# A four-level wavelet layer: input rows dealt four to a partition, and the forward transform split into 32x32 TensorE tiles over four images at once

## What is computed

```
def _L0_conv_ref(x, w_yl, w_yh):
    yl, yh = _dwt2(x, 4)
    yl_out = jnp.einsum('bixy,ioxy->boxy', yl, w_yl)
    yh_out = yh[:-1] + [jnp.einsum('bicxy,iocxy->bocxy', yh[-1], w_yh)]
    return _idwt2(yl_out, yh_out)
```

## Time and profile before

| | us |
|---|---|
| median of 3 runs | 2176.98 (2175.05 to 2181.13) |
| the profiled execution | 2176.45 |
| its span, first to last instruction | 2174.7 |
| last image's `h_stage` begins | 760.85 |
| first step of the mix begins | 773.15 |
| first store of the second pass | 885.15 |

### The profile page before, as it was taken

How to read it: one execution, slowest core, us unless ns; L and a number is a source line. 1 busy time by engine, 2 the same in 40 slices (tenths; PEclk the granted TensorE clock), 3 DMA queues, 4 the chain that set the end, 5 groups by cost and what they waited for, 6 DMA issues and landing times.

```text
span 2174.7 us, 30813 instructions
## 1 busy us (share of the span) xinstructions
PE 2006.3 (92%) x10540; PEld 824.1 (38%) x10540; DVE 846.7 (39%) x1615; ACT 506.2 (23%) x1079; POOL 3.6 (0%) x7
## 2 busy tenths in 40 slices
PE   8999999999999967999989889889889889889886
PEld 3344343434434345444333333333333333333332
DVE  2222222222222233455544444444444444444443
ACT  2222222222222268212112112112112112112110
POOL 0000000000000000000000000000000000000000
PEclk9999999999999989999999999999999999999998
DMA  9999999999999968699999999999999999999999
GB/s 382 409 363 361 346 357 360 349 363 347 356 353 352 349 244 316 246 384 408 409 409 409 409 409 409 409 409 409 409 409 409 409 409 409 409 409 409 408 409 396
DMA packets 406629, 827.10 MB, mean 380 GB/s; under 512 B 12752, under 2 KB 13520, under 8 KB 406608
## 3 DMA queue, kind: packets, MB, share of 16 engines
q1 hardware_dynamic: 406608, 826.80, 100.9%
HBM read 558.32 MB, written 268.44 MB: 380 GB/s over the span
## 4 chain that ended last, share of the span: by engine, by line
DMA 48%; PE 8%; SPq 5%; issue 2%; ACT 1%; DVEq 0%; ACTq 0%; DVE 0%
DMA out<-x_sb 46%; PE ps L455 5%; SPq L278 5%; PE ps L445 1%; DMA both<-w_full 1%; ACT both L541 1%; PE ps L411 1%; DMA x_sb<-x 1%; DMA both<-w_rest 1%; PE ps L406 0%; PE ps L435 0%; SPq L273 0%; ACT mix_sb L548 0%; SPq L272 0%; DVEq L134 0%
## 5 line engine op out<-in xcount | busy, mean ns | idle before, releaser
L455 PE MATMUL ps<-spread,const 128*128 128x512 f32 x2048 | 940.9, 602 | 111.2 <-DVE x_sb L690 111.2
L690 DVE TENSOR_TENSOR x_sb<-ps,x_sb 128x1024 f32<-128x1024 f32 x500 | 592.4, 1221 | 668.2 <-DMA x_sb<-x 593.3
L455 PEld LDWEIGHTS ps<-spread,const 128*128 128x128 f32 x2048 | 372.4, 189 | 679.2 <-issue 402.2
L327 PE MATMUL ps<-x_sb,const 128*64 128x512 f32 x2048 | 495.0, 604 | 8.8 <-DMA x_sb<-x 8.8
L595 ACT COPY spread<-ps 84x512 f32<-84x512 f32 x256 | 149.0, 582 | 970.1 <-PE ps L445 969.7
L646 DVE COPY work<-ps 128x80 f32<-128x80 f32 x256 | 61.9, 242 | 560.2 <-PE ps L337 560.2
L494 ACT COPY work<-ps 128x512 f32<-128x512 f32 x256 | 150.2, 587 | 537.4 <-PE ps L327 537.4
L445 PE MATMUL ps<-const,pick 128*84 128x512 f32 x512 | 261.3, 592 | 0.7 <-issue 0.7
L327 PEld LDWEIGHTS ps<-x_sb,const 128*64 128x64 f32 x2048 | 130.0, 137 | 205.9 <-issue 189.7
L337 PEld LDWEIGHTS ps<-const,work 128*128 128x128 f32 x1024 | 107.0, 140 | 207.2 <-issue 206.1
L337 PE MATMUL ps<-const,work 128*128 128x128 f32 x1024 | 167.8, 286 | 0.1
(11 more groups left out here) (22 smaller groups left out, 262.7 us busy)
## 6 DMA issues: line engine op xcount, KB each, us to landing
x_sb<-x SPq DMA_DIRECT2D x498, 1024.0 KB, 12.6
out<-x_sb SPq DMA_DIRECT2D x250, 1024.0 KB, 13.2
both<-w_full SPq DMA_DIRECT2D x30, 896.0 KB, 6.5
work<-x SPq DMA_DIRECT2D x6, 1024.0 KB, 9.9
out<-work SPq DMA_DIRECT2D x6, 1024.0 KB, 11.7
both<-w_rest SPq DMA_DIRECT2D x6, 224.0 KB, 3.9
const<-consts SPq DMA_DIRECT2D x1, 912.0 KB, 4.7
```

The source lines that it names most:

```text
L327: last = nc.tensor.matmul(ps[64 * j:64 * j + 64, p], const[:, AH + 64 * k:AH + 64 * k + 64], x_sb[:, c, k], start=k % 2 == 0, stop=k % 2 == 1)
L455: last = nc.tensor.matmul(ps[:, 2 + k], const[:, SH + P * k:SH + P * k + P], spread[:, p], start=True, stop=True)
L690: nc.vector.tensor_tensor(part, ps[:, 2 + 2 * half:4 + 2 * half], part, ALU.add).then_inc(added[half], 1)
```

## The change

- An image lies in SBUF as [128, 4, 512] with rows 4 p to 4 p + 3 in partition p. The four rows are adjacent in HBM too, so that each load and store of an image moves one run of 8 KB to a partition. In the built program the access is `[[2048, 128], [1, 2048]]` on both sides, the same form as the weight loads have. The constants of the second pass (`SH`) are dealt to match; its code is otherwise the same.
- `h_stage(a, t)` handles four images at once. It applies only the first three levels (low-pass) along the height, where 128 rows of input touch at most 25 outputs. So each 32-partition group g of the array takes its own 128 rows, and each 32-column group another image m: 64 matmuls of 32 rows by 32 columns, streaming 512. Output of (g, m) goes to PSUM quadrant (g + m) mod 4 of bank m.
- `turn_stage` is now a product instead of a transpose: along_h (128x128 as weights) times the fourth level's matrix `A4` (84 columns streamed). It turns the data, and sums the four windows in PSUM. VectorE's four instructions become one copy.
- `w_stage` applies three levels along the width: four matmuls of 32 columns, streaming 336, once for four images. VectorE copies the result (`copy_w`), and the new `last_stage` applies the fourth level (one matmul, 84 columns of weights, 336 streamed) into another bank.
- The waits change with it. `h_stage` waits for four loads and for four `copy_h`; SP waits once for four slots, then issues four loads; `copy_h` runs four in a row, and `copy_c` behind them. In the mix VectorE makes three quarters of the diagonal operand and ScalarE one, since the rows of the coefficients are no longer cut in two halves.

```diff
-    x_rows = x.rearrange("b i (c p) w -> (b i) p c w", p=P)
-    out_rows = out.rearrange("b i (c p) w -> (b i) p c w", p=P)
+    x_rows = x.rearrange("b i (p r) w -> (b i) p r w", r=ROW_RUN)
+    out_rows = out.rearrange("b i (p r) w -> (b i) p r w", r=ROW_RUN)
...
                 for c in range(SLOTS):
-                    sp.wait_ge(h_done[c], t)
+                    if c % GROUP == 0:
+                        sp.wait_ge(h_done[c // GROUP], t)
                     sp.dma_start(x_sb[:, c], x_rows[SLOTS * t + c]).then_inc(x_loaded[c], 16)
...
+            def h_stage(a, t):
+                n = HALVES * t + a
+                for m in range(GROUP):
+                    pe.wait_ge(x_loaded[GROUP * a + m], 16 * (t + 1))
+                pe.wait_ge(h_copied, GROUP * n)
+                pe.sem_inc(h_begun, 1)
+                for r in range(ROW_RUN):
+                    for g in range(SEGS):
+                        part = slice(TILE * g, TILE * g + TILE)
+                        for m in range(GROUP):
+                            to = TILE * ((g + m) % SEGS)
+                            last = nc.tensor.matmul(ps[to:to + TILE, m], const[part, A3H + TILE * r:A3H + TILE * r + TILE],
+                                                    x_sb[part, GROUP * a + m, r], start=r == 0, stop=r == ROW_RUN - 1)
+                last.then_inc(h_done[a], 1)
+            def turn_stage(a, t, m):
+                n = GROUP * (HALVES * t + a) + m
+                pe.wait_ge(h_copied, n + 1)
+                if m >= 2:
+                    pe.wait_ge(t_copied, n - 1)
+                else:
+                    pe.wait_ge(t_copied, GROUP * (HALVES * t + a))
+                for k in range(SEGS):
+                    last = nc.tensor.matmul(ps[:, 4 + m % 2, ROWS * k:ROWS * k + ROWS], along_h[:, m, P * k:P * k + P],
+                                            const[:, A4 + ROWS * m:A4 + ROWS * (m + 1)], start=True, stop=True)
+                last.then_inc(t_done, 1)
+            def w_stage(n, after=None):
+                pe.wait_ge(t_copied, GROUP * n + GROUP)
+                if after is not None:
+                    pe.wait_ge(m_copied, STEPS * after + STEPS)
+                for k in range(SEGS):
+                    at = A3W + TILE * k
+                    last = nc.tensor.matmul(ps[TILE * k:TILE * k + TILE, 6, 0:GROUP * ROWS], const[:, at:at + TILE],
+                                            turned[:, k].rearrange("p m r -> p (m r)"), start=True, stop=True)
+                last.then_inc(w_done, 1)
+            def last_stage(n):
+                pe.wait_ge(w_copied, n + 1)
+                pe.wait_ge(c_copied, n)
+                nc.tensor.matmul(ps[0:ROWS, 7, 0:GROUP * ROWS], const[:, A4:A4 + ROWS], third,
+                                 start=True, stop=True).then_inc(c_done, 1)
...
             def turn1(t, first=False, batch=None):
+                for a in range(HALVES):
+                    n = HALVES * t + a
+                    h_stage(a, t)
+                    before = not first or a > 0
+                    if before:
+                        w_stage(n - 1, after=batch if a else None)
+                    turn_stage(a, t, 0)
+                    if before:
+                        last_stage(n - 1)
+                    for m in range(1, GROUP):
+                        turn_stage(a, t, m)
...
+            def copy_h(a, t, m):
+                act.wait_ge(h_done[a], t + 1)
+                nc.scalar.copy(along_h[:, m], ps[:, m]).then_inc(h_copied, 1)
...
-                for q in range(Q // 2, Q):
+                for q in range(Q - 1, Q):
...
-                for q in range(Q // 2):
+                for q in range(Q - 1):
```

More of the change, by code:

```diff
@@ L83, in synthesis, with low @@
     return m
-def transforms():
+def low(levels):
     a, s, sizes = np.eye(SIZE), np.eye(SIZE), [SIZE]
-    for _ in range(LEVELS - 1):
+    for _ in range(levels):
         a = analysis(sizes[-1], LO) @ a
@@ L92, in transforms @@
         sizes.append(a.shape[0])
[L93 to L99, removed]
+    return a, s, sizes[-1]
+A3H, A4, A3W = 0, 128, 464
+SW, SH, EYE, NEG = 592, 1104, 1616, 1744
 CONSTS = NEG + 32
 def constants():
-    a, s = transforms()
+    a, s, n = low(LEVELS - 1)
+    last = np.concatenate([analysis(n, t) for t in (LO, HI)])
+    back = np.concatenate([s @ synthesis(COEFS, t)[:n] for t in (LO, HI)], axis=1)
     c = np.zeros((P, CONSTS))
[L110 to L120, removed]
+    for g in range(SEGS):
+        part = slice(TILE * g, TILE * g + TILE)
+        near = slice(STEP3 * g, STEP3 * g + NEAR)
+        for r in range(ROW_RUN):
+            at = A3H + TILE * r
+            c[part, at:at + NEAR] = a[near, P * g + r:P * g + P:ROW_RUN].T
+        for m in range(GROUP):
+            turned = TILE * ((g + m) % SEGS)
+            c[turned:turned + NEAR, A4 + ROWS * m:A4 + ROWS * (m + 1)] = last[:, near].T
+        at = A3W + TILE * g
+        c[:, at:at + NEAR] = a[near, P * g:P * g + P].T
+    c[:ROWS, SW:SW + SIZE] = back.T
+    for r in range(ROW_RUN):
+        c[:ROWS, SH + P * r:SH + P * r + P] = back[r::ROW_RUN].T
     c[:, EYE:EYE + P] = np.eye(P)
@@ L318, in _ @@
             pe.wait_ge(const_loaded, 16)
[L320 to L329, removed]
@@ L364, in channels_stage @@
                     h = Q * (4 * v + n)
-                    last = nc.tensor.matmul(ps[:, 6 + v % 2, P * n:P * n + P],
-                                            coef[:, h:h + Q].rearrange("p q i -> p (q i)"),
-                                            const[:, EYE:EYE + P], start=True, stop=True, is_transpose=True)
+                    last = nc.tensor.matmul(ps[:, 6 + v % 2, P * n:P * n + ROWS],
+                                            coef[0:ROWS, h:h + Q].rearrange("p q i -> p (q i)"),
+                                            const[0:ROWS, EYE:EYE + ROWS], start=True, stop=True, is_transpose=True)
                 last.then_inc(m_done, 1)
             def turn1(t, first=False, batch=None):
-                for c in range(SLOTS):
-                    h_stage(c, t)
-                    if c:
-                        turn_stage(c - 1, t)
-                    elif not first:
-                        turn_stage(SLOTS - 1, t - 1)
-                    if c == 1 and not first:
-                        w_stage(1, t - 1)
-                    if c == 5:
-                        w_stage(0, t)
-                    if batch is not None and 3 <= c <= 5:
-                        channels_stage(2 * (c - 3), batch)
-                        channels_stage(2 * (c - 3) + 1, batch)
+                for a in range(HALVES):
[9 more added lines that the diff above has]
+                        turn_stage(a, t, m)
+                        if batch is not None and a == 0:
+                            channels_stage(2 * m - 2, batch)
+                            channels_stage(2 * m - 1, batch)
             turn1(0, first=True)
@@ L391, in _ @@
                     turn1(TURNS_BATCH * b + r)
-            turn_stage(SLOTS - 1, TURNS - 1)
-            w_stage(1, TURNS - 1)
+            w_stage(HALVES * TURNS - 1)
+            last_stage(HALVES * TURNS - 1)
             for v in range(STEPS):
```

144 lines of the change are left out of this document (62 added, 82 removed).

## The result

The changed kernel takes **2112.57 us** in the median of four runs (2077.18, 2104.13, 2121.01, 2158.54) against 2177.06 for the kernel before. Two of the four, 2121.01 and 2158.54, lie over 1.5% above the fastest and count as slow runs, so the ratio, 0.960 with a 95% interval of 0.949 to 0.971, compares the other two, whose median is 2090.66 us. By it the kernel is faster, as forecast, but by 86 us and not by 171. The four scatter over 81 us, where those of before lie within 6. The profiled execution is the fastest of them, 2077.18 us.

A forecast was written before the change was run, and what follows sets the result against it. First pass taken as bound by TensorE, second by the DMA, the mix by ScalarE with weights close behind. From 2176.45: first pass -118, mix -5, second pass -48, together -171, giving 2005 us; range 1980 to 2095.

The forecast's parts named there:

- The second pass, -48 us: Second pass, DMA-bound: 8 KB packets at 308 ns, 425 GB/s instead of 409, for 498 loads and stores, -48 us.
- Rival A: Both passes: long runs bring nothing, DMA stays at 409 GB/s; first pass -93, second 0, total 2079 us; chance 0.12.
- The first pass, -118 us: First pass: becomes DMA-bound at 2.467 us an image, so the mix begins at 655 instead of 773.15, -118 us.
- Bound: First pass: the bound moves from TensorE to the DMA, four loads taking 9.87 us against 9.2, 7% to spare.
- h_stage: First pass, TensorE: 16 tiles run side by side, instructions no limit at about 10 ns each; 3.7 us.
- Turning: First pass, turn_stage: 8 pairs of weight load and matmul, hidden behind each other, 0.11 us a pair, 0.95 a turning.
- Rival B: First pass stays TensorE-bound, weight loads not hidden (1.4 us a turning) or dearer hand-overs; total 2101; 0.13 with halfway cases.
- Rival C: First pass: row groups do not work side by side, h_stage takes 13.8 us, total 2609 us, slower; chance 0.07.
- Round: First pass: TensorE takes 8.95 us for four images, 9.2 with the channel turnings of each eighth round averaged in.
- Start: First rounds of the first pass: more code must be fetched; the idle loads hide it, or it costs some us.
- Tail: End of the first pass: one round and the work behind it before the mix, 17 us against 12 before.
- The mix, -5 us: Mix: ScalarE falls to 1.5 us a step, weights need 2.15 to 2.25, against 2.54; between 0 and -10, taken -5.

The follow-up runs named there:

- align: The changed kernel with 192 unused bytes a partition behind the constants, so that x_sb starts at byte 8448, a multiple of 256: 2023.07 us, ratio 0.930.
- tile2k_align: The changed kernel's tiled first pass, but with 2 KB runs as before, and 192 unused bytes behind the constants: 2092.25 us, ratio 0.961.
- after_again: The changed kernel, unchanged, measured and profiled a second time: 2097.36 us, ratio 0.957.
- resync: The changed kernel, but SP waits four times in the second pass until all it has issued has landed: 2057.53 us, ratio 0.943.

## Why the prediction was right and wrong

**That the range held the result is luck.** Its upper end, 2095, was set to take in rivals A and B. Neither happened, and what cost the changed kernel its gain stands in no rival.

**The second pass, -48 us: the size was right, and the changed kernel did not get it.** In its profile the pass is 1.5 us shorter than before. The line through the packet rows gave 308 ns and 425 GB/s; the trace has 309 ns and 427, and align, with the bad start address taken away, has -50.5. The step that failed is the price of a packet: 308 ns from its length alone, put as one rate ("I take 425") on the whole second pass, loads and stores alike. The address had no term in the sum. Where `x_sb` starts at a multiple of 256, loads alone and loads with stores do run alike, at 427; at 8256 loads alone run at 422, and with stores at 427 until 1310 us and then, in episodes, at 361 to 394. A 1.5% slower packet on one engine of 16 was no 1.5% loss: its lag added up over hundreds of transfers, and from then on the rate was down by 8 to 15% in the episodes. The prediction also read the diff for instructions and access patterns, and not for where tensors come to lie; the new length of the constants stood in it. The 2090.66 - 2023.07 = **67.6 us** between the changed kernel and align are four fifths of the 86 us that the forecast missed.

**Rival A, 2079 us**, comes close to the profiled time of 2077.18, for the wrong reason. Long runs do bring their gain (427 against 409, and 2092 against 2023 us between tile2k_align and align); it was lost elsewhere. The Trainium skill's 408.7 GB/s for 4 KiB rows ("DMA: Bandwidth & Descriptors", section on the iDMA fabric) isn't borne out here: 4 KB runs moved 420, 8 KB runs 427.

**The first pass, -118 us**, became -98.3, and -107.1 in align (mix at 666.0).
- *Bound.* It moved to the DMA, as forecast. Align's rounds are at 427 GB/s, and TensorE still waits 0.3 to 0.4 us in each.
- *h_stage* took 4.45 us, not 3.7. The step "instructions are no limit, about 10 ns each" failed. In the records the first 16 start 7.5 ns apart in the mean, most later ones 16 to 17 with holes of 0.19 us, and 16 large instructions take 3.64 where 64 small ones take 4.45: 17 ns for each pair more. The price came from weight loads and matmuls of 32 columns in the mix, with 10 ns on average over a burst; it did not carry over.
- *Turning.* Records of 8 in 1.12 us and 24 in 2.80, 0.117 a pair, as taken (0.11). Rival B is refuted, with its 1.4 us a turning.
- *Rival C* is refuted: 4.45 us, not 13.8, with four row groups writing four quadrants of one PSUM bank at once. The rule of the Trainium skill that the prediction weighed ("TensorEngine Tiling (Array Packing)", Gotcha 1) is not borne out by this trace, where 4 x 4 tiles with a quadrant each run together.
- *Round.* TensorE alone needs 9.40 us (rounds without a wait), not 8.95, and 10.92 with channel turnings; with one of these in eight it is 9.59, and against 9.81 for four loads the slack is 2%, not 7%.
- *Start.* "The idle loads hide it, or it costs some us" was the soft step. The loads had no such reserve (align's slices 1 to 3 are at 357, 406 and 383), and the start cost 15 us against steady rounds. *Tail*, from the last round's start to the mix: forecast 17, measured 17.8 (17.4 in align).

**The mix, -5 us**, was 0 (109.4 us, 109.1 before). The prediction named the next limit, the weights at 2.15 to 2.25 us a step, but priced them at full rate. They come at about 2.45 a step, and 11% of their packets run long. The DMA's share is 0.94 in align's mix (690 to 750 us), so its queue runs empty at times; whether the three buffers are the reason was not tried.

With the place set right, as in align, what is left of the miss is small and divides so: 2005 + 11 (mix begins at 666) + 5 (no gain in the mix) - 2.5 (second pass) = 2018.5, where its profiled execution took 2018.63.

## What to carry to other kernels

Read a diff for the sizes of small tensors too: here 192 bytes in a table of constants decided some 68 of 154 us. Start what a full-rate DMA moves at a multiple of 256 bytes in the partition, and look at single packets, not only at GB/s. Where transfers wait for each other's last landing, look at how far apart the landings of one transfer are: here the last one's lag added up over the kernel. A flat rate in the first hundreds of microseconds didn't show it, and a rare drain was a cheap test for it.

## What the runs showed of the hardware that was not expected

- The start address in SBUF: with `x_sb` 64 bytes past a multiple of 256, packets in a stream of loads are 4 to 5 ns longer on average, at 2 KB (84 to 88.2) and at 8 KB (309 to 313.7), and at 8 KB 128 bytes past do the same (313.6). Loads alone then run at 387 in place of 409 GB/s with 2 KB runs, and at 422 in place of 427 with 8 KB. In a stream of loads and stores about 5% of the packets are longer, and one landing of 16 falls behind.
- From the rates: 2, 4 and 8 KB packets cost an engine 80, 156 and 307 ns (409, 420, 427 GB/s), which is about 4.5 ns and 0.037 ns a byte.
- Where the lag grew to 8 us and more, the time scattered: the changed kernel's runs spread over 4% (2% in after_again), those of align over 0.6% and of resync over 0.3%.
